# Weight remainders by accumulating DMA, work of VectorE's opening moved, and products moved ahead of the masked transposes, in a sparse-attention and mixture-of-experts kernel

## The reference

```python
# stage 1, sparse attention pattern added to a layernorm
sim = einsum('bhnd,bhmd->bnm', Q, K) / (sqrt(d) * H)        # Q, K: ctx @ Wq.T, ctx @ Wk.T
threshold = top_k(sim, 76)[0][:, :, -1:]                    # of 256 values a row
A = sigmoid(sim) * (sim >= threshold)
A = (A + swapaxes(A, -1, -2)) * 0.5
x = x + (1 - gamma) * layernorm(x) + gamma * A              # gamma = sigmoid(gamma_raw)
# stage 2, mixture of 8 experts, best 2 of each token
x_ = layernorm(x); combine = top-2 softmax scores of x_ @ gate_w, times alpha
h = gelu(x_ @ fc1_w[e] + fc1_b[e]);  y = h @ fc2_w[e] + fc2_b[e]
x = x + sum over e of y * combine[:, e]
```

## Time and profile before

| | us |
|---|---|
| median of 3 runs (137.95 to 138.25) | 138.05 |
| the profiled execution's own time | 137.94 |
| its span (first to last instruction) | 136.2 |
| PE busy / weight loads | 121.4 / 110.5 |
| DVE / ACT / POOL busy | 102.3 / 83.4 / 72.2 |

### The profile page before, as it was taken

The page is one execution under the profiler, slowest core; times in us unless marked ns, Lnnn a source line. Parts: engine busy times, 40 slices in busy tenths (PEclk is TensorE's granted clock), DMA queues, the critical chain, the costliest instruction groups (busy, mean ns, idle before and its releaser), DMA issues.

```text
span 136.2 us, 2763 instructions
## 1 busy us (share of the span) xinstructions
PE 121.4 (89%) x904; PEld 110.5 (81%) x904; DVE 102.3 (75%) x401; ACT 83.4 (61%) x207; POOL 72.2 (53%) x69
## 2 busy tenths in 40 slices
PE   6796989999429998999879999996999999999990
PEld 4433756899339988999779999995999999999990
DVE  0078898989999819899997879999976526943472
ACT  3188789799055746865399487663954645445620
POOL 2046656989908997565029735430594334454300
PEclk9999999999986999999999999999999999999999
DMA  2999940000000000001100000020000002000002
GB/s 63 218 397 415 413 162 0 0 5 2 0 0 0 5 0 0 2 0 44 38 2 2 0 5 0 2 77 2 5 0 0 5 0 77 0 0 5 2 0 77
DMA packets 2516, 6.90 MB, mean 51 GB/s; under 512 B 300, under 2 KB 772, under 8 KB 2500
## 3 DMA queue, kind: packets, MB, share of 16 engines
q1 hardware_dynamic: 2500, 6.71, 13.8%
HBM read 5.66 MB, written 1.05 MB: 49 GB/s over the span
## 4 chain that ended last, share of the span: by engine, by line
PE 49%; DVE 32%; issue 6%; POOL 6%; ACT 4%; DVEq 0%; POOLq 0%
PE p_y L473 21%; PE p_h L451 19%; DVE acc L1054 7%; DVE picked L1011 4%; POOL w_lo L660 3%; DVE left L873 3%; DVE above L835 2%; PE p_y L354 2%; DVE left L884 2%; ACT h_act L568 2%; DVE comb L1016 1%; DVE weight L1014 1%; POOL rstd L649 1%; PE p_a L378 1%; DVE guess L829 1%
## 5 line engine op out<-in xcount | busy, mean ns | idle before, releaser
L681 POOL TENSOR_TENSOR h_lo<-h_act,h_hi 128x512 fp32r<-128x512 f32 x31 | 40.7, 1317 | 43.9 <-ACT h_hi L576 28.9
L568 ACT ACTIVATE h_act<-p_h,small_sb 128x256 f32<-128x256 f32 x64 | 26.7, 469 | 20.1 <-PE p_h L451 19.8
L451 PE MATMUL p_h<-xt_hi,w_hi 128*128 128x256 f32 x128 | 33.2, 282 | 0.1
L451 PE MATMUL p_h<-xt_hi,w_lo 128*128 128x256 f32 x128 | 33.0, 280 | 0.0
L473 PE MATMUL p_y<-w_hi,h_hi 128*128 128x256 f32 x126 | 26.4, 291 | 6.9 <-DVE acc L1054 6.9
L1054 DVE SCALAR_TENSOR_TENSOR acc<-p_y,comb,acc 128x256 f32<-128x256 f32 x55 | 24.0, 476 | 11.3 <-PE p_y L473 10.2
L473 PEld LDWEIGHTS p_y<-w_hi,h_hi 128*128 128x128 f32 x126 | 19.4, 191 | 7.6 <-issue 7.4
L451 PE MATMUL p_h<-xt_lo,w_hi 128*128 128x256 f32 x128 | 25.5, 280 | 0.0
L473 PE MATMUL p_y<-w_lo,h_hi 128*128 128x256 f32 x126 | 25.4, 284 | 0.0
L473 PE MATMUL p_y<-w_hi,h_lo 128*128 128x256 f32 x126 | 25.4, 284 | 0.0
L451 PEld LDWEIGHTS p_h<-xt_hi,w_hi 128*128 128x128 f32 x128 | 24.4, 191 | 0.4 <-issue 0.4
(11 more groups left out here) (140 smaller groups left out, 182.9 us busy)
## 6 DMA issues: line engine op xcount, KB each, us to landing
w_sb<-w SPq DMA_DIRECT2D x8, 512.0 KB, 8.0
x_sb<-x SPq DMA_DIRECT2D x1, 768.0 KB, 8.3
out<-acc SPq DMA_DIRECT2D x3, 256.0 KB, 2.5
x_sb<-x SPq DMA_DIRECT2D x1, 256.0 KB, 4.6
out<-acc SPq DMA_DIRECT2D x2, 128.0 KB, 2.0
attn_sb<-attn SPq DMA_DIRECT2D x1, 192.0 KB, 5.0
small_sb<-small SPq DMA_DIRECT2D x1, 97.5 KB, 4.6
attn_sb<-attn SPq DMA_DIRECT2D x1, 96.0 KB, 2.3
```

The source lines that it names most:

```text
L451: last = nc.tensor.matmul(dst, w_[:, e, 0, k, c * P:(c + 1) * P], v[:, b % 2, k, :], start=n == 0, stop=n == len(trio) - 1)
L568: last = nc.scalar.activation(h_act[:, s % 2, c], tiled(p_h[s % 2])[:, c, :], ACT.Gelu, bias=b1_sb[:, e, c:c + 1])
L681: nc.gpsimd.tensor_tensor(h_lo[:, s % (LAG + 1)], h_act[:, s % 2], h_hi[:, s % (LAG + 1)], ALU.subtract).then_inc(h_lo_ready, 1)
```

## The change

Experts 0 and 1 keep their subtraction on POOL. For experts 2 to 7 ACT now writes minus `w_hi` into `w_lo` (`weight_neg`), and POOL issues a DMA (`weight_rest`) that reads the weights from HBM once more and adds them to it; `up` waits for its landing, and the wait in `down` goes. POOL makes `w_hi` of six experts and ACT of two. DVE's two halves of `w_lo` go. In the opening, the small inputs are loaded second instead of fourth, the gamma terms are computed at DVE's start, `ln1_affine(0)` goes to POOL, `ln1(1)` goes from ahead of `residual(0)` to step 1, and the flags are one instruction for both tiles instead of two, `missed` with a tensor in the place of a scalar pointer. PE's `sim_of(2)` and `sim_of(3)` go behind the masked transposes, with 13 constant products ahead of these and 8 instead of 18 ahead of the transposes of `xn`. POOL's wait for `masked` goes. In the loop, `guesses`, `middle_guess`, `spread_of`, `signs_of`, `signs_again_of`, `better_guess` with its count, and `drop_eight` go to earlier places. Left out of the diff are declarations, the two helpers that `better_guess` is split into, and changes of waits that only follow from these.

```diff
-POOL_HI = 2
+POOL_HI = (0, 1, 2, 5, 6, 7)
+ACT_HI = (3, 4)
+POOL_HI_AT = {0: 6, 2: 7}
-WARM_BEFORE_XN = 18
+WARM_BEFORE_MASK = 13
+WARM_BEFORE_XN = 8
...
-                for b in range(2, BATCHES):
-                    sim_of(b)
...
-                    pe.wait_ge(w_lo_ready[e][0], 1)
+                    if e < 2:
+                        pe.wait_ge(w_lo_ready[e][0], 1)
+                    else:
+                        pe.wait_ge(w_rest_in[e], 16)
...
+            keep_warm(WARM_BEFORE_MASK)
             transpose_masked(0)
+            for b in range(2, BATCHES):
+                sim_of(b)
             keep_warm(WARM_BEFORE_XN)
...
+            def weight_neg(e):
...
+                nc.scalar.activation(w_lo[:, e], w_hi[:, e], ACT.Copy, scale=-1.0).then_inc(w_neg_ready, 1)
...
             u_copy(0)
+            act.wait_ge(small_in, 16)
+            nc.scalar.activation(gam[:, 0:1], gamma_sb, ACT.Tanh, scale=0.5).then_inc(gam_th, 1)
+            nc.scalar.activation(gate_parts[:, :, 0], gate_sb, ACT.Copy).then_inc(gate_hi_ready, 1)
...
             sigmoid(0)
-            weight_hi(POOL_HI)
-            for b in range(1, BATCHES):
+            weight_hi(3)
+            sim_copy(1)
+            spread_of(1)
+            weight_neg(2)
+            weight_neg(3)
+            for b in range(2, BATCHES):
                 sim_copy(b)
...
             signs_of(1)
             xt_hi_of(0)
             signs_again_of(1)
+            weight_hi(4)
...
+                if s < 2:
+                    weight_neg(4 + s)
+                if s in (1, 3):
+                    weight_neg(6 + s // 2)
...
+            def weight_rest(e):
+                pool.wait_ge(w_neg_ready, e - 1)
+                nc.gpsimd.dma_start(w_lo[:, e], w[:, e].bitcast(F32R), accum_op=ALU.add).then_inc(w_rest_in[e], 16)
...
             weight_lo(0, 0)
-            weight_hi(1)
+            ln1_affine(0)
             base(0)
-            weight_lo(1, 0)
             pool.wait_ge(gate_hi_ready, 1)
...
-            pool.wait_ge(masked, TILES)
-            weight_lo(0, 1)
-            weight_lo(2, 0)
+            weight_hi(1)
+            weight_hi(2)
+            weight_lo(1, 0)
+            weight_rest(2)
             rstd(veps2, rstd2, 0, ln2_veps, ln2_rstd)
             pool.wait_ge(xn_ready, TILES)
-            weight_lo(3, 0)
+            weight_lo(0, 1)
+            weight_rest(3)
             weight_lo(1, 1)
-            weight_lo(4, 0)
+            weight_hi(5)
             for s in range(STEPS):
...
                     hidden_lo(s)
-                if s == 0:
+                if s == 1:
                     rstd(veps1, rstd1, 1, ln1_veps, ln1_rstd)
-                    weight_lo(2, 1)
...
+                if s < 4:
+                    weight_rest(4 + s)
+                if s in POOL_HI_AT:
+                    weight_hi(POOL_HI_AT[s])
...
                     if t == TILES - 1:
-                        flag_missed(b)
+                        if b == 0:
+                            flag_few(b)
                     step_of_tile(nc.vector.scalar_tensor_tensor(left[:, t], above[:, t], REPLACED, sim_of_tile(b, t),
                                                                 ALU.mult, ALU.add))
+                flag_missed(b)
...
-            flag_few(0)
-            gamma_terms()
+            offset_again(0, 0)
+            second_guess(0, 0)
+            offset_again(0, 1)
+            count_above(0, 0)
+            second_guess(0, 1)
+            count_above(0, 1)
             drop_above(0)
-            ln1_affine(0)
             take_eight(0)
...
             add_masked(0)
-            ln1(1)
             residual(0)
...
                 if s == 1:
+                    ln1(1)
                     combine(0)
+                if more and e == 1:
                     drop_eight(0)
...
-                if s == 3:
-                    weight_lo(DVE_SPLITS[0])
```

More of the change, by code:

```diff
@@ L208, in xattn_moe_program @@
         u_ready = sem("u_ready")
+        w_neg_ready = sem("w_neg_ready")
+        w_rest_in = [sem(f"w_rest_in{e}") for e in range(EXPERTS)]
         rows_cleared = sem("rows_cleared")
@@ L457, in down @@
                 b, e = divmod(s, EXPERTS)
-                if b == 0:
+                if b == 0 and e < 2:
                     pe.wait_ge(w_lo_ready[e][1], 1)
@@ L669, in base, with ln1_affine @@
                 last.then_inc(base_ready, 1)
+            def ln1_affine(b):
+                pool.wait_ge(gam_ready, 1)
+                pool.wait_ge(ln1_agg, (b + 1) * TILES)
+                pool.wait_ge(ln1_rstd, b + 1)
+                for t in range(TILES):
+                    nc.gpsimd.tensor_scalar(mul1[:, b, t:t + 1], rstd1[:, b, t:t + 1], gam[:, 2:3], ones[:], ALU.mult,
+                                            ALU.add)
+                    last = nc.gpsimd.tensor_scalar(add1[:, b, t:t + 1], mv1[:, b, t, 0:1], gam[:, 3:4],
+                                                   rstd1[:, b, t:t + 1], ALU.mult, ALU.mult)
+                last.then_inc(ln1_mul, 1)
             def add_masked(b):
@@ L789, in gamma_terms @@
                 dve.wait_ge(gam_ready, 1)
[L791 to L794, removed]
             def sim_copy(t):
@@ L831, in better_guess @@
                                         ALU.subtract).then_inc(better_ready, 1)
+            def better_guess(b, t):
+                offset_again(b, t)
+                second_guess(b, t)
             def count_above(b, t):
@@ L838, in flag_few @@
             def flag_few(b):
[L840 to L843, removed]
+                dve.wait_ge(counted, (b + 1) * TILES)
+                nc.vector.tensor_scalar(few[:], count[:], TOP_K - WINDOW, None, ALU.is_lt).then_inc(few_ready, 1)
             def flag_missed(b):
@@ L848, in flag_missed @@
                     dve.wait_ge(missed_sum, b)
-                for t in range(TILES):
-                    dve.wait_ge(few_ready, b * TILES + t + 1)
-                    nc.vector.tensor_scalar(missed[:, t:t + 1], count[:, t:t + 1], TOP_K, few[:, t:t + 1],
-                                            ALU.is_ge, ALU.add).then_inc(missed_ready, 1)
+                dve.wait_ge(few_ready, b + 1)
+                nc.vector.scalar_tensor_tensor(missed[:], count[:], TOP_K, few[:], ALU.is_ge,
+                                               ALU.add).then_inc(missed_ready, 1)
             steps = [0]
@@ L1079, in _ @@
                 middle_guess(0, t)
-            for t in range(TILES):
-                better_guess(0, t)
-                count_above(0, t)
-            flag_few(0)
-            gamma_terms()
+            offset_again(0, 0)
[4 more added lines that the diff above has]
+            count_above(0, 1)
             drop_above(0)
-            ln1_affine(0)
             take_eight(0)
@@ L1106, in _ @@
                 more = nxt < BATCHES
-                if more and b and e == 0:
-                    for t in range(TILES):
-                        middle_guess(nxt, t)
-                if more and e == (1 if b else 0):
+                if more and e == 0:
                     for t in range(TILES):
@@ L1116, in _ @@
                     drop_above(nxt)
-                if b < BATCHES and e == (2 if b else 0):
-                    top2(b)
+                if s == 0:
+                    top2(0)
                 if more and e == 1:
@@ L1121, in _ @@
                 if s == 1:
+                    ln1(1)
                     combine(0)
+                if more and e == 1:
                     drop_eight(0)
-                if b and b < BATCHES and e == 2:
+                if 0 < b < BATCHES and e == 2:
+                    top2(b)
                     combine(b)
-                if more and b and e == 2:
-                    drop_eight(0)
                 if more and e == 2:
@@ L1135, in _ @@
                     mask(nxt)
-                if s == 3:
-                    weight_lo(DVE_SPLITS[0])
-                if s == 4:
+                if s == 6:
                     b2_parts_of()
-                    weight_lo(DVE_SPLITS[1])
                 if more and e == 5:
                     residual(nxt)
+                if e == 5 and nxt + 1 < BATCHES:
+                    guesses(nxt + 1)
                 if more and e == 6:
@@ L1146, in _ @@
                     comb_parts_of(b)
+                if e == 7 and nxt + 1 < BATCHES:
+                    for t in range(TILES):
+                        middle_guess(nxt + 1, t)
                 if more and e == 7:
                     xt_lo_of(nxt)
-                if e == EXPERTS - 1 and nxt + 1 < BATCHES:
-                    guesses(nxt + 1)
+                if e == 7 and nxt + 1 < BATCHES:
                     ln1(nxt + 1)
```

52 lines of the change are left out of this document (21 added, 31 removed).

## The result

The changed kernel took 140.44 us (median of 9 runs, 138.51 to 140.84) beside 138.05 us (9 runs, 137.95 to 138.25) of the kernel before: a ratio of 1.012 (1.008 to 1.017), slower by 1.2%. Some executions of a kernel are slower than the rest (here two of nine), and in this document ratios compare the fast ones (a median of 139.89 us for the changed kernel), while a time given with its range is the median of all runs. 129.7 us was predicted, and 134.3 us was the range's upper end. The profiled execution took 140.57 us, its span is 138.8 us.

What follows compares the result with a forecast made beforehand. PE was taken to bound the kernel, interrupted by DVE, whose search sets PE's start before 24.2 us. Terms -2.9 - 1.76 - 0.8 - 2.1 - 0.7 = -8.3 us gave a 127.9 us span, 129.7 us forecast, range 128.0 to 134.3.

Steps and rivals of the forecast that it cites:

- First stop: PE's wait for DVE's addition 0, behind `up(4)`: about 1.3 us instead of 4.2, so -2.9 us.
- I take one blocked instruction, 1.3 us, between none and four (5.2 us): In the first stop, the delay DVE was still expected to suffer from POOL's remaining work: 1.3 us.
- Clock behind the stop: After a first stop of only 1.3 us, PE's clock was expected not to fall: -1.76 us.
- `xn(1)`: From 50.7 us on, PE's stop goes since `w_lo` no longer stands ahead of `rstd` on POOL: -0.8 us.
- Stops in batches 1 and 2: PE's waits at the third steps shrink from 2.6 to 0.5 us as search work moves: -2.1 us.
- Opening: Before `up(0)`: maxima 1.1 us earlier, offset by `choose` blocked 1.1 us; `ln1(1)` out of `residual`'s way leaves -0.7 us.
- at 2.4 GHz 1.9 us and 8 products 0.9: PE's two similarities and constants behind the masked transposes, done at 21.9 us when `xn` is.
- the rival called the clock: Opening: clock not up for the similarities, PE 2 us late for `xn`; +3.5 us, 133.2 us; chance 0.22.
- DMAs: POOL's six adding transfers: issue 1.0 us each, landing after 4.4 us, in time for `up`; nothing added.
- the rival of late DMAs: Landings after 8.0 us, POOL's issuing included, make PE wait at experts 3 to 5; 134.7 us, chance 0.12.
- Slower than before: The adding itself sets the pace, deciding from landings of about 12 us; 141 us at 13 us; chance 0.06.
- It does not do what it says: `xn` no earlier, picks in lockstep with POOL's copies, first stop keeps 3 us; 132 us; no chance of its own.

Runs made afterwards that it cites:

- e3: Changed kernel without the six added transfers, remainder left out, `up` waiting for the negation alone; 131.16 us, ratio 0.952 to the kernel before.
- e5: Changed kernel with POOL waiting for its own last result after copies and `h_lo` in the first five steps and ahead of the loop; 133.49 us.
- e2: Changed kernel with the six transfers issued by SP as plain loads into a spare tensor, remainder left out; 131.16 us.
- e6: Kernel before with only the moves of search work inside the loop; 135.99 us, ratio 0.986.
- e11: Second try (e10) with 16 constants instead of 22 and POOL waiting for the end of `choose` between its copies of experts 1 and 2; 131.95 us.
- e1: Changed kernel with PE's order of before: similarities 2 and 3 ahead of the masked transposes, no constants there, 18 behind; 138.92 us.
- e7: Changed kernel with 22 instead of 13 constant products ahead of the masked transposes; 138.82 us, ratio 1.007 to the kernel before.
- e9: Changed kernel with POOL's waits for its own results (as e5) and 22 constants ahead of the masked transposes; 134.27 us.
- e4: Changed kernel with POOL's copies for experts 6 and 7 moved from steps 0 and 2 to ahead of the loop; 135.16 us.
- e10: e9 with ACT negating straight from `w_sb` and each adding DMA from expert 4 on issued one place earlier; 132.32 us.
- e8: Changed kernel with PE's opening order of before, POOL's copies of experts 5 to 7 ahead of the loop, waits behind `h_lo` alone; 135.46 us.

## Why the prediction was wrong

The ledger against the predicted span of 127.9 us: `up(0)` 2.7 us late (26.20 for 23.5), the first stop 5.2 longer (6.5 for 1.3), the clock behind it (2.90 + 2.16 for 2 x 1.42) 2.2, the wait for a landing 0.5. That is 10.6 of 10.9 us.

*First stop, predicted -2.9, measured +2.3.* **This is the step that failed**: "I take one blocked instruction, 1.3 us, between none and four (5.2 us)", and with it the terms for the issues, "I take 1.0, six times, on a POOL that lost more", and "Nothing is added". The 1.0 us was right: the issues last 0.88 to 1.18 us. What was wrong is that one of them costs DVE at most itself. DVE lost 3.08 - 0.17 on `best_f`, 2.94 - 0.87 on the picks and 2.86 - 0.17 on `weight`, 7.7 us, because the run of POOL's instructions behind an issue is closed to such work. The rule of one turn between two POOL instructions was read from a trace without a POOL DMA and carried to a stretch with four. e3 (no issue: about 9 us back) and e5 (waits between: about 7 us back, everything else kept) show it; e2 excludes plain transfers, and e5, which keeps the adding ones, excludes these as what holds DVE.

*Clock behind the stop, predicted -1.76, measured +0.5* (2.22 for 1.76): it follows the stop, 6.5 us without a product.

*`xn(1)`, predicted -0.8*: right, no wait of PE is left there, and DVE's for `rstd` is 0.5 us at its longest for 3.0.

*Stops in batches 1 and 2, predicted 2.6 to 0.5*: right, 0.6 in the changed kernel; alone (e6) it brings 2.0 us.

*Opening, predicted -0.7, measured +2.0.* The terms of DVE were right: the maxima 1.16 us earlier; `choose` was held 1.7 us (0.84 + 1.30 for 0.22 each) where 1.1 was taken, within its bounds. `xn` was there at 22.26 us, near the 21.9 predicted. The Trainium skill's rule ("SBUF — State Buffer", "Who interferes with whom") fell due here, and e11 shows its price by taking it away. The wrong term was PE's, "at 2.4 GHz 1.9 us and 8 products 0.9": the similarities took 3.7 us and the constants 1.9, at 1.2 GHz. That is the rival called the clock, given 0.22, and its size (2 us late for `xn`) was right: 24.88 for 22.63 (22.26 and half of the 0.74). Its 3.5 us on the end was not: the first `up` already ran at 2.4 GHz, and e1 and e7, which bring the clock earlier, gained 1.1 to 1.6.

*DMAs.* Landing after 5.6 us, between 4.4 and the upper bound of 8.0, cost one wait of 0.5 us. The Trainium skill's fit that the prediction cited ("DMA: Bandwidth & Descriptors", "Anatomy of one DMA — SWDGE (gpsimd) path"), an estimate of 3.2 us without the adding, lies below the 5.6 us, and below the 3.9 us of e2's plain loads too, which SP issued. In e5, where DVE isn't late, the landings cost 1.9 us. So the rival of late DMAs was true in a small part, and its sentence on POOL's issuing pointed at the right place and the wrong direction: it had DVE keeping POOL, where POOL kept DVE.

*Slower than before*, given 0.06, came true in its sign alone, which is luck: for it a landing would have had to take 12 us. "It does not do what it says" had picks in lockstep with copies at 132 us, the nearest to what happened, and was still priced by single turns.

## What to carry to other kernels

A DMA issued by POOL is not only its own microsecond: look what DVE does, down to casts of four columns and flags of two, while POOL's following instructions run, and give POOL a wait for its own result between them, or issue from SP where nothing has to be added. Work saved ahead of such a hold is in part given back to it (2.7 us earlier brought 1.1 to 1.6, or nothing in e9), so clear the hold first. One-column instructions were not held, so joining two of them into one of two columns can cost more than it saves; no run kept the flags apart, so that price is argued and not measured. A rule of turns read from one mix of instructions holds for that mix.

## What the runs showed that was not expected

Behind a DMA issue POOL's instructions overlap in the records, and DVE's casts and tensor_scalars of two columns and more, and its work with both inputs in SBUF, get no turn for two to five of them: 1.6 us (`comb` in e4) to 4.8. Not held were one-column work and work with an input in PSUM (`xt_lo` of the changed kernel, 0.42 and 0.41 us from 26.09 us on, beside POOL's subtraction and copy). One-input work is held too: `best_f` (3.08 us for 0.17), `few` (3.57 and 4.18 us for 0.17). The Trainium skill, "SBUF — State Buffer", section "Who interferes with whom", says that whoever issues first has the shared ports "for the whole instruction", and that a cast or tensor_scalar can, under conditions, take them as well; the held cast agrees with the second, while the runs show a hold of several instructions, not of one. Its remark that a DVE operation can stall a DMA issued by GpSimd has the reverse here. Why the run is closed stays open: that a wait of POOL for itself opens it is shown, the mechanism is not, nor what ends a run without one. In e4 `few` came free at 30.46 us though the next issue had begun at 30.11 and `h_lo` followed at 30.73; in e7 `comb` did not at the same kind of place (37.55). Whether an adding DMA lands later for the adding or for being issued by POOL was not told apart (5.6 us; a plain load from SP 3.9).

The clock. 13 constants, a pause of 1.85 us and 4 us of similarities left it at 1.2 GHz; 16 and 22 constants, with a pause of 0.5 us or none, brought it before the similarities (four records of similarities in 1.13 us in e10, in 2.07 us in the changed kernel). In e4, again with 13 constants, it came at 16.9 us and was gone again at 20.3, while similarities ran back to back. The changed kernel's scatter, 2.3 us where the kernel before has 0.3, fits a clock on such an edge, and so do the others: the five kernels with 13 constants, this one included, scatter by 1.6 to 2.8 us, the five with 16 or 22 by 0.2 to 0.8. Against it stands e1, without any there, with 2.6 us in ten runs (e8, with the same order of PE, has 0.4 in four). No trace shows a fastest run, so the cause of the scatter stays open.
